# Stage-1 and stage-2 attention on one Trainium2 core: both halves of q and k are copied first, tokens are prepared a unit sooner, their transpose is issued first

## The chip, the cores and the metric

The kernel runs on 1 core of one Trainium2 chip. The metric is the device time of one execution in microseconds (us). A core has TensorE (PE, with its weight loads as PEld), VectorE (DVE), ScalarE (ACT), GpSimd (POOL) and SyncE (SP), which here only issues DMAs. Each engine takes its own instructions strictly in order; engines wait for one another through semaphores.

## The reference

```python
x = x + tanh(g_xattn[0]) * L0_xattn(layernorm(x), ctx)   # 8 heads of 64
x = x + tanh(g_ffn[0])   * L0_ffn(layernorm(x))          # 16 experts, chosen by a Sinkhorn affinity
x = x + tanh(g_xattn[1]) * L1_xattn(layernorm(x), ctx)   # 16 heads of 64
x = x + tanh(g_ffn[1])   * L1_ffn(layernorm(x))          # 2 of 8 experts for each of the 128 samples
# xattn: q = x Wq, k = ctx Wk, v = ctx Wv; softmax(q k^T / 8) v; then Wo and a bias
```

x is 128 samples of 64 tokens of 128 floats, the context 128 x 64 x 96. All is float32.

## The kernel before

A tile is two samples: 128 tokens on the 128 partitions, 64 tiles in all. The program has four parts in a row: the first attention, the expert layer, the second attention and the routed layer. The change lies in the function `attention`, which builds the first and the second attention. In the first (`first` is true) a tile is one unit, 64 units. In the second a tile is two units of eight heads each (G = 2), 128 units; keys come from DRAM, where the expert layer has left them (`keys_ahead`), and the first half of the program has also left the transposed context there (`context_T`).

Each engine runs `body(j)` for j in order. `Unit(j, k)` is the unit j - k, so a positive k is a unit that started k steps ago and a negative k one that is prepared ahead. A unit `opens` if it is the first of its tile: each unit of the first attention, each second one of the second. What the engines do in step j, in their order:

- PE: project q (and in the first attention k) of unit j in two parts (`U0`, `U1`, each in a PSUM bank of its own), V of unit j-2, output product Y of j-5, attention times V (O) of j-4, scores S of unit j. S(j) waits for the copy of q and k (`uc1`, or `uc0` in the second attention) and for `sub` of j-1. For the second attention there is one part.
- ACT: copy of O (j-5); copy of the first part of q and k (j); high half of V (`vh`, j-2); exp (j-1), which waits for `sub`; copy of the second part of q and k (j); high half of the probabilities (`phi`, j-2); then, for the tile of unit j+3, the layer norm (`ln`, into `xn`) and its high half in f16 (`xh`, into `parted[..., 0]`).
- DVE: sum over exp (`den`, j-2) and its reciprocal (`rden`); maximum (`top`) and difference (`sub`) of the scores j-1; low half of V (`vl`, j-2), after `vh`; low half of the normed tokens (`xl`, tile of j+2); in the first attention the high half of the context (`chi`, j+3); the residual (`res`, j-5); norm statistics; in six steps of each of three stretches of the first attention also a part of the arithmetic of the norm (`norm`, stages 0 to 5).
- POOL: probabilities times `rden` (`mul`, j-2); bias added to x; a share of the expert weights' split (first attention); low half of the probabilities (`plo`, j-2), after `phi`; low half of the context (`clo`, tile of j+2).
- SP, in order: weight and input loads of the first attention; store of `context_T`; keys and context of unit j+1 (second attention); transpose of the probabilities `PT` of j-2, which waits for `plo`; transpose of the tokens (`transpose_tokens`, L505 to L512) of j+2, which waits for `xl`, in the first attention also for `clo`.

The values are split into a high and a low f16 half (hi + lo), and products run as three passes. The transposed tokens land in `XT`; PE waits for them (semaphores `xc`) before U of an opening unit. `XT` and `parted` have 4 slots in the first attention and 2 in the second, `xn` has 2. The line of ACT's copies is L640, that of a helper, whatever they copy.

Of the kernel before, what the change touches and what calls it, by code (L numbers as in the profile page):

```python
# [103 lines left out]
def _build(nc, whole, I, out):  # L104
# [190 lines left out]
    def attention(tag, G, Wq, Wk, Wv, Wo, bo, gate, ew=None, rw=None, routing=None):  # L295

        first = ew is not None
        U = NT * G
        INNER = 512 * G
        s = Sems(tag)  # L300
        with ExitStack() as c:
# [148 lines left out]
            with nc.Block() as block:  # L450
                @block.sync
                def _(e):
                    def body(j):
                        a, a2, nx, soon = (Unit(j, k) for k in (0, 2, -1, -2))
                        if first and a.on and a.par == 0:
                            turn = a.j.mod(4)
                            if turn == 0 and a.j.off > 0:
                                n = a.j.div(4)
                                wait(e, s["ew_lo"], n, 2, -2)
                                load_w2(e, n)  # L460
                            elif turn == 2 and (a.j + 2).inside(U):
                                n = (a.j - 2).div(4) + 1
                                wait(e, s["ew_lo"], n, 2, -3)
                                load_w1(e, n)
                        if first and 2 <= j.off < 10:
                            part = 16 * (j.off // 6 + 2)
                            four = slice(4 * j.off + 24, 4 * j.off + 28)
                            e.dma_start(x[:, four, :], xv[:, four, :]).then_inc(s[f"x{part}"], 16)
                            e.dma_start(ctx32[:, four, :], cv[:, four, :]).then_inc(s[f"c{part}"], 16)
                        if first and 24 <= j.off < 24 + NE:  # L470
                            n = j.off - 24
                            with nc.allow_non_contiguous_dma("a small bias, transposed once"):
                                e.dma_start(ew.b1T[:, FT * n:FT * n + FT],
                                            I["L0_ffn_b1"][n].rearrange("(k p) -> p k", p=P)).then_inc(s["b1"], 16)
                        if a.opens and first:
                            on_slot(e, "xc", a)
                            e.dma_start(context_T[bass.ds(a.t.value, 1)].rearrange("o p k -> p (o k)"),
                                        XT[0:DC, a.slot, 2:4].rearrange("p h t -> p (h t)"))\
                             .then_inc(s[f"stored{a.slot}"], 16)
                        if nx.opens and not first and nx.j.off > 0:  # L480
                            load_keys(e, nx)
                            load_context(e, nx)
                        if a2.on:
                            wait(e, s["plo"], a2.j)
                            wait(e, s["O"], a2.j - 2)
                            e.dma_start_transpose(PT[:, a2.par].rearrange("p h k t -> p (h k) t"),
                                                  Ph[:, a2.par].rearrange("p h k t -> p (h k t)"))\
                             .then_inc(s[f"pt{a2.par}"], 16)
                        if soon.opens and (first or soon.j.off > 0):
                            transpose_tokens(e, soon)  # L490
                        if rw is not None:
                            if 8 <= j.off < 18:
                                rw.load_small(e, j.off - 8)
                            if 18 <= j.off < 18 + 2 * NE1:
                                rw.load_expert(e, (j.off - 18) // 2, j.off % 2)
# [18 lines left out]
                    def load_keys(e, a):  # L514
                        wait(e, s["S"], a.j - 3)
                        e.dma_start(KL1[:, a.tp].rearrange("p k l -> p (k l)"),
                                    keys_ahead[bass.ds(a.t.value, 1)].rearrange("o p k -> p (o k)"))\
                         .then_inc(s[f"ul{a.tp}"], 16)
# [115 lines left out]
                @block.scalar  # L634
                def _(e):
                    def body(j):
                        a, a1, a2, a5, later = (Unit(j, k) for k in (0, 1, 2, 5, -3))

                        def copy(to, frm):
                            return e.activation(to, frm, ACT.Copy)  # L640
# [14 lines left out]
                            copy(O32[:, a5.par], psO[:, :, 0:256]).then_inc(s["oc"], 1)  # L655
                        if a.on:
                            projected(0)
                        if a2.on:
                            wait(e, s["V"], a2.j)
                            wait(e, s["O"], a2.j - 4)  # L660
                            copy(vB[:, a2.four, 0].rearrange("p b k -> p (b k)"), psV[:]).then_inc(s["vh"], 1)
                        if a1.on:
                            wait(e, s["sub"], a1.j)
                            e.activation(E[:, a1.four], E[:, a1.four], ACT.Exp, bias=zero_col[:], scale=DH ** -0.5)\  # L664
                             .then_inc(s["exp"], 1)
                        if a.on and first:
                            projected(1)
                        if a2.on:
                            wait(e, s["mul"], a2.j)
                            wait(e, s[f"pt{a2.par}"], turn_of(a2.j, 2, a2.par) - 1, 16)  # L670
# [4 lines left out]
                        if later.opens:  # L675
                            wait(e, s["xl"], later.t - 2)
                            e.activation(xn[:, later.tp, :], tile_of(later.t, x), ACT.Identity, bias=column_of(later.t, nmr),
                                         scale=column_of(later.t, rstd)).then_inc(s["ln"], 1)
                            on_slot(e, "xc", later, -1)
                            wait(e, s["ln"], later.t)  # L680
                            copy(parted[:, later.slot, 0, :], xn[:, later.tp, :]).then_inc(s["xh"], 1)
                    if first:
                        parts = (0, 8, 16, 32, 48, U)
                        for part, (lo, hi) in enumerate(zip(parts, parts[1:])):
                            e.wait_ge(s["nmr"], part + 1)
                            pipeline(e, body, lo - 3, hi - 3, max(lo - 3, 8), hi - 3, 4)
                        for j in range(U - 3, U + 5):
                            body(Step(None, 0, j))
                    else:
                        for name in ("ln", "xh"):  # L690
                            e.sem_inc(s[name], 1)
                        pipeline(e, body, -1, U, 8, U - 3, 4)
                        for j in range(U, U + 5):
                            body(Step(None, 0, j))
                            if j < U + 3:
                                routing["scalar"](e, j - U, psQK[:, 1, :])

                @block.gpsimd
                def _(e):
                    def body(j):  # L700
                        a, a2, soon = (Unit(j, k) for k in (0, 2, -2))
                        if a2.on:
                            wait(e, s["rden"], a2.j)
                            e.tensor_tensor(E[:, a2.four], E[:, a2.four],  # L704
# [28 lines left out]
                    if rw is not None:  # L733
                        rw.clear(e)
                    if first:
                        pipeline(e, body, -2, U + 2, 8, U - 2, 4)
                    else:
                        routing["clear"](e)
                        pipeline(e, body, 0, U + 2, 8, U, 4)
                        routing["gpsimd"](e)  # L740

                @block.vector
                def _(e):
                    def body(j, ahead=()):
                        a, a1, a2, a5, soon, later = (Unit(j, k) for k in (0, 1, 2, 5, -2, -3))
                        by_head = "p (k h) n -> p h k n"

                        if a2.on:
# [19 lines left out]
                        if soon.opens and (first or soon.j.reg is not None or soon.j.off > 0):  # L768
                            wait(e, s["xh"], soon.t)
                            e.tensor_tensor(parted[:, soon.slot, 1, :], xn[:, soon.tp, :], parted[:, soon.slot, 0, :],  # L770
                                            ALU.subtract).then_inc(s["xl"], 1)
                        if first and later.on:
                            on_slot(e, "xc", later, -1)
                            e.tensor_copy(parted[:, later.slot, 2, 0:DC], tile_of(later.t, ctx32)).then_inc(s["chi"], 1)
                        if a5.closes:
                            wait(e, s["Y"], a5.j)
# [16 lines left out]
                    if first:  # L793
# [4 lines left out]
                                    body(Step(i, 4, lo + u), ahead)  # L798

                        e.wait_ge(s["c0"], 16)  # L800
                        for j in range(-3, 0):
                            body(Step(None, 0, j))
                        e.wait_ge(s["x8"], 16)
                        for j in range(4):
# [8 lines left out]
                        for part, lo in ((2, 8), (3, 24), (4, 40)):  # L813
# [4 lines left out]
                                e.wait_ge(s["c48"], 64)  # L818
                            for j in range(lo, lo + NORM_STAGES):
                                body(Step(None, 0, j), (24,) if j < 40 else ())  # L820
                                for stage in ((0, 1), (2,), (3,), (4,), (5,), ())[j - lo]:
                                    norm(part, slice(lo + 8, lo + 24), stage)
                            if lo < 40:
                                for j in range(lo + 6, lo + 8):
# [5 lines left out]
                    else:  # L830
# [3 lines left out]
                        e.wait_ge(s["stats"], 8)  # L834
                        queue_norm(e, s, lnt, 0, late)
                        queue_shift(e, s, 0, late, nmr)
                        e.sem_inc(s["xl"], 1)
                        pipeline(e, body, -1, U, 8, U - 3, 4)
                        pa, pb = psQK[:, 1, :], psS[:, 0, :]
                        routing["vector"](e, -1, pa, pb)  # L840
                        for j in range(U, U + 5):
# [1321 lines left out]
```

## Time and profile before

| | us |
|---|---|
| median of 3 runs | 2038.03 (2034.89 to 2048.37) |
| the profiled execution | 2044.66, its span 2042.9 |
| busy in the span: PE, DVE, ACT, POOL | 1785.4, 1554.4, 1553.0, 671.9 |
| TensorE's granted clock, mean | 0.966 of full speed |

The first attention runs from about 16 to 350 us of the span, the expert layer to about 1370, the second attention to about 1895, the routed layer to the end. Busy shares are means over stages with different limits. "Idle before" an instruction with a releaser says what ended the wait of its engine. Start times and durations of successive instructions on one engine overlap a little, since the next starts while the last drains.

### The profile page before, as it was taken

Reading aid. Unit: us, or ns where it says so; the run is one execution under the profiler, and the core shown is the slowest. Engines: PE = TensorE matmul, PEld = TensorE weight load, DVE = VectorE, ACT = ScalarE, POOL = GpSimd, SP = SyncE. Lnnn points to the kernel's source line nnn. Section 1 sums busy time; section 2 is a strip of 40 time slices with the busy share of each in tenths; the row PEclk is TensorE's granted clock in tenths of the full one; section 3 lists DMA queues with packets and bytes.
Section 4 is the critical chain, followed back from the end, with each engine's and each line's share of the span. In section 5 each row is a group of like instructions: output and inputs, shape, how many; then the busy total and the mean of one; then the engine's idle time right before and its main releaser. Section 6 shows DMA issues by size and latency. Waiting matters only on the chain. (4 is left out here: it accounts for less than half of the span.)

```text
span 2042.9 us, 95028 instructions
## 1 busy us (share of the span) xinstructions
PE 1785.4 (87%) x39513; PEld 1389.3 (68%) x39513; DVE 1554.4 (76%) x3645; ACT 1553.0 (76%) x2637; POOL 671.9 (33%) x921
## 2 busy tenths in 40 slices
PE   3788888788799999999999999967888888888798
PEld 3777777534366666666666666757777777777687
DVE  4788887579688888888888888765777777777654
ACT  3687877466699999999999998856777777777443
POOL 3677777442000000000000000014555555555465
PEclk8899999799799999999999999988999999999799
DMA  6755555379200000000000001005665555555233
GB/s 158 146 114 112 119 113 113 101 270 372 71 13 14 12 14 12 14 12 14 12 14 12 14 12 52 2 24 118 150 156 139 137 141 139 138 146 142 68 114 114
DMA packets 371233, 185.79 MB, mean 91 GB/s; under 512 B 290366, under 2 KB 350822, under 8 KB 371046
## 3 DMA queue, kind: packets, MB, share of 16 engines
q1 hardware_dynamic: 370198, 182.55, 34.4%
q8 instruction: 123, 2.02, 0.4%
q10 hardware_dynamic: 848, 0.71, 0.1%
q14 instruction: 64, 0.52, 0.1%
HBM read 68.95 MB, written 42.86 MB: 55 GB/s over the span
## 5 line engine op out<-in xcount | busy, mean ns | idle before, releaser
L1646 DVE TENSOR_TENSOR h<-g,h 128x1024 f16<-128x1024 f32 x256 | 313.4, 1224 | 137.9 <-ACT h L1571 137.6
L245 PEld LDWEIGHTS psE<-ew,h 128*128 128x128 f16 x6144 | 350.9, 98 | 56.0 <-issue 40.1
L245 PE MATMUL psE<-ew,h 128*128 128x128 f16 x6144 | 365.0, 219 | 12.8 <-DVE eo L1656 6.0
L1566 ACT ACTIVATE g<-psH,eb1T 128x512 f32<-128x512 f32 x512 | 330.3, 680 | 30.5 <-PE psH L245 24.1
L723 POOL TENSOR_TENSOR Ph<-E,Ph 128x512 f16<-128x512 f32 x192 | 222.4, 1159 | 304.1 <-ACT Ph L640 304.1
L1586 POOL TENSOR_TENSOR shared<-shared 128x128 f16<-128x128 f32 x1 | 0.4, 428 | 846.6 <-ACTq L1387 846.6
L1571 ACT ACTIVATE h<-g 128x1024 f16<-128x1024 f32 x256 | 270.6, 1057 | 8.1
L704 POOL TENSOR_TENSOR E<-E,rden 128x512 f32<-128x512 f32 x192 | 200.0, 1042 | 51.2 <-DVE rden L753 50.6
L562 PE MATMUL psQK<-shared 128*64 128x128 f16 x3072 | 114.6, 226 | 76.6 <-DMA shared<-shared 71.6
L245 PE MATMUL psH<-shared,ew 128*128 128x512 f16 x768 | 178.6, 383 | 0.0
L245 PE MATMUL psH<-xg,ew 128*128 128x512 f16 x768 | 176.9, 380 | 0.0
L765 DVE TENSOR_TENSOR vB<-psV,vB 128x512 f16<-128x512 f32 x128 | 88.0, 687 | 107.7 <-ACT vB L640 107.3
L640 ACT ACTIVATE QK<-psQK 128x512 f32<-128x512 f32 x128 | 76.4, 597 | 106.1 <-PE psQK L562 106.0
L664 ACT ACTIVATE E<-E,zero_col 128x512 f32<-128x512 f32 x192 | 137.5, 716 | 22.6 <-DVE E L760 22.1
L562 PEld LDWEIGHTS psQK<-shared 128*64 128x64 f16 x3072 | 93.5, 113 | 89.6 <-DMA shared<-shared 41.1
L590 PE MATMUL psY<-shared 128*64 128x128 f32 x2048 | 137.7, 278 | 5.1 <-ACT shared L640 5.1
L751 DVE TENSOR_REDUCE den<-E 128x8 f32<-128x512 f32 x192 | 129.8, 676 | 13.7 <-ACT E L664 12.1
L760 DVE TENSOR_TENSOR E<-psS,top 128x512 f32<-128x512 f32 x192 | 132.8, 692 | 9.7
L757 DVE TENSOR_REDUCE top<-psS 128x8 f32<-128x512 f32 x192 | 127.2, 663 | 13.6 <-PE psS L622 13.5
L245 PEld LDWEIGHTS psH<-shared,ew 128*128 128x128 f16 x768 | 70.3, 98 | 93.6 <-issue 19.0
L245 PEld LDWEIGHTS psH<-xg,ew 128*128 128x128 f16 x768 | 69.9, 98 | 89.9 <-issue 12.7
L640 ACT ACTIVATE shared<-psO 128x512 f32<-128x512 f32 x192 | 112.4, 586 | 16.1 <-PE psO L607 10.4
(284 smaller groups left out, 3810.9 us busy)
## 6 DMA issues: line engine op xcount, KB each, us to landing
keys_ahead<-shared SPq DMA_DIRECT2D x64, 512.0 KB, 4.9
shared<-keys_ahead SPq DMA_DIRECT2D x64, 512.0 KB, 3.8
rawe<-in_L_ffn_w_dram SPq DMA_DIRECT2D x32, 256.0 KB, 3.1
wb<-rw SPq DMA_DIRECT2D x64, 128.0 KB, 2.0
rows<-places SPq DMA_DIRECT2D x110, 64.0 KB, 2.6
out_dram<-x SPq DMA_DIRECT2D x7, 512.0 KB, 3.2
context_T<-shared SPq DMA_DIRECT2D x64, 48.0 KB, 2.4
PT<-Ph SPq DMA_TRANSPOSE x192, 3.4
```

What stands on the lines that cost most here:

```text
L245: last = e.matmul(to, a, b, start=start and n == 0, stop=stop and n == 2, **flags)
L562: last = e.matmul(psQK[half(m), bank, P * q:P * q + P], w[0:rows, wl, a.g, k, half(m)], moving[:, ml, :], start=n == 0, stop=n == 2)
L590: last = e.matmul(psY[half(b), 0:D], O32[:, a5.par, hp, P * k2 + 64 * b:P * k2 + 64 * b + 64], wo[:, a5.g, k2, hp, :], start=a5.g == hp == ...
L640: return e.activation(to, frm, ACT.Copy)
L664: e.activation(E[:, a1.four], E[:, a1.four], ACT.Exp, bias=zero_col[:], scale=DH ** -0.5)\
L704: e.tensor_tensor(E[:, a2.four], E[:, a2.four], rden[:, a2.par, :].unsqueeze(2).broadcast_to([P, 8, N]), ALU.mult)\
L723: e.tensor_tensor(Ph[:, a2.par, 1].rearrange("p k t -> p (k t)"), E[:, a2.four].rearrange("p h l -> p (h l)"), Ph[:, a2.par, 0].rearrange( ...
L751: e.tensor_reduce(den[:, a2.par, :], E[:, a2.four], AX.X, ALU.add).then_inc(s["den"], 1)
L760: e.tensor_tensor(E[:, a1.four].rearrange(by_head, h=2), scores, top[:].unsqueeze(3).broadcast_to([P, 2, 4, N]), ALU.subtract).then_inc(s[ ...
L1566: e.activation(g32[:, ft, :], psH[:, ft, :], ACT.Gelu_apprx_tanh, bias=b1T[:, a.expert(1) * FT + ft:a.expert(1) * FT + ft + 1]).then_inc(s ...
L1571: e.activation(h[:, 1 - par, 0, ft - 1:ft + 1, :], g32[:, ft - 1:ft + 1, :], ACT.Copy).then_inc(s["h_hi"], 1)
L1646: e.tensor_tensor(h[:, 1 - par, 1, 2 * q:2 * q + 2, :], g32[:, 2 * q:2 * q + 2, :], h[:, 1 - par, 0, 2 * q:2 * q + 2, :], ALU.subtract)\
```

## The change

- ACT copies the second part of q and k right behind the first (first attention), ahead of `vh` and exp.
- Layer norm (`ln`) on ACT is made for the tile of j+4 in place of j+3. Its high half `xh` moves from ACT to DVE: it stands behind `xl` in DVE's step and waits for the `ln` of the same step number. `chi` also goes to j+4, `xl` and `clo` to j+3.
- SP issues the transpose of the tokens of j+2 at the head of its step, ahead of loads, store and `PT`. The keys of the second attention are loaded for j+2 and still ahead of `PT`, the context for j+1 behind it.
- The last two stages of the norm's arithmetic are done in one step. Loops and start counts are shifted to match.

```diff
@@ -451,7 +451,9 @@
                 @block.sync
                 def _(e):
                     def body(j):
-                        a, a2, nx, soon = (Unit(j, k) for k in (0, 2, -1, -2))
+                        a, a2, soon = (Unit(j, k) for k in (0, 2, -2))
+                        if soon.opens and (first or soon.j.off > 0):
+                            transpose_tokens(e, soon)
                         if first and a.on and a.par == 0:
                             turn = a.j.mod(4)
                             if turn == 0 and a.j.off > 0:
@@ -477,17 +479,17 @@
                             e.dma_start(context_T[bass.ds(a.t.value, 1)].rearrange("o p k -> p (o k)"),
                                         XT[0:DC, a.slot, 2:4].rearrange("p h t -> p (h t)"))\
                              .then_inc(s[f"stored{a.slot}"], 16)
-                        if nx.opens and not first and nx.j.off > 0:
-                            load_keys(e, nx)
-                            load_context(e, nx)
+                        if soon.opens and not first:
+                            load_keys(e, soon)
                         if a2.on:
                             wait(e, s["plo"], a2.j)
                             wait(e, s["O"], a2.j - 2)
                             e.dma_start_transpose(PT[:, a2.par].rearrange("p h k t -> p (h k) t"),
                                                   Ph[:, a2.par].rearrange("p h k t -> p (h k t)"))\
                              .then_inc(s[f"pt{a2.par}"], 16)
-                        if soon.opens and (first or soon.j.off > 0):
-                            transpose_tokens(e, soon)
+                        nx = Unit(j, -1)
+                        if nx.opens and not first and nx.j.off > 0:
+                            load_context(e, nx)
                         if rw is not None:
                             if 8 <= j.off < 18:
                                 rw.load_small(e, j.off - 8)
@@ -634,7 +636,7 @@
                 @block.scalar
                 def _(e):
                     def body(j):
-                        a, a1, a2, a5, later = (Unit(j, k) for k in (0, 1, 2, 5, -3))
+                        a, a1, a2, a5, later = (Unit(j, k) for k in (0, 1, 2, 5, -4))
 
                         def copy(to, frm):
                             return e.activation(to, frm, ACT.Copy)
@@ -655,6 +657,8 @@
                             copy(O32[:, a5.par], psO[:, :, 0:256]).then_inc(s["oc"], 1)
                         if a.on:
                             projected(0)
+                            if first:
+                                projected(1)
                         if a2.on:
                             wait(e, s["V"], a2.j)
                             wait(e, s["O"], a2.j - 4)
@@ -663,8 +667,6 @@
                             wait(e, s["sub"], a1.j)
                             e.activation(E[:, a1.four], E[:, a1.four], ACT.Exp, bias=zero_col[:], scale=DH ** -0.5)\
                              .then_inc(s["exp"], 1)
-                        if a.on and first:
-                            projected(1)
                         if a2.on:
                             wait(e, s["mul"], a2.j)
                             wait(e, s[f"pt{a2.par}"], turn_of(a2.j, 2, a2.par) - 1, 16)
@@ -676,20 +678,16 @@
                             wait(e, s["xl"], later.t - 2)
                             e.activation(xn[:, later.tp, :], tile_of(later.t, x), ACT.Identity, bias=column_of(later.t, nmr),
                                          scale=column_of(later.t, rstd)).then_inc(s["ln"], 1)
-                            on_slot(e, "xc", later, -1)
-                            wait(e, s["ln"], later.t)
-                            copy(parted[:, later.slot, 0, :], xn[:, later.tp, :]).then_inc(s["xh"], 1)
                     if first:
                         parts = (0, 8, 16, 32, 48, U)
                         for part, (lo, hi) in enumerate(zip(parts, parts[1:])):
                             e.wait_ge(s["nmr"], part + 1)
-                            pipeline(e, body, lo - 3, hi - 3, max(lo - 3, 8), hi - 3, 4)
-                        for j in range(U - 3, U + 5):
+                            pipeline(e, body, lo - 4, hi - 4, max(lo - 4, 8), hi - 4, 4)
+                        for j in range(U - 4, U + 5):
                             body(Step(None, 0, j))
                     else:
-                        for name in ("ln", "xh"):
-                            e.sem_inc(s[name], 1)
-                        pipeline(e, body, -1, U, 8, U - 3, 4)
+                        e.sem_inc(s["ln"], 1)
+                        pipeline(e, body, -2, U, 8, U - 4, 4)
                         for j in range(U, U + 5):
                             body(Step(None, 0, j))
                             if j < U + 3:
@@ -698,7 +696,7 @@
                 @block.gpsimd
                 def _(e):
                     def body(j):
-                        a, a2, soon = (Unit(j, k) for k in (0, 2, -2))
+                        a, a2, soon = (Unit(j, k) for k in (0, 2, -3))
                         if a2.on:
                             wait(e, s["rden"], a2.j)
                             e.tensor_tensor(E[:, a2.four], E[:, a2.four],
@@ -733,7 +731,7 @@
                     if rw is not None:
                         rw.clear(e)
                     if first:
-                        pipeline(e, body, -2, U + 2, 8, U - 2, 4)
+                        pipeline(e, body, -3, U + 2, 8, U - 3, 4)
                     else:
                         routing["clear"](e)
                         pipeline(e, body, 0, U + 2, 8, U, 4)
@@ -742,7 +740,7 @@
                 @block.vector
                 def _(e):
                     def body(j, ahead=()):
-                        a, a1, a2, a5, soon, later = (Unit(j, k) for k in (0, 1, 2, 5, -2, -3))
+                        a, a1, a2, a5, soon, later = (Unit(j, k) for k in (0, 1, 2, 5, -3, -4))
                         by_head = "p (k h) n -> p h k n"
 
                         if a2.on:
@@ -769,8 +767,11 @@
                             wait(e, s["xh"], soon.t)
                             e.tensor_tensor(parted[:, soon.slot, 1, :], xn[:, soon.tp, :], parted[:, soon.slot, 0, :],
                                             ALU.subtract).then_inc(s["xl"], 1)
+                        if later.opens and (first or later.j.reg is not None or later.j.off > 0):
+                            wait(e, s["ln"], later.t)
+                            on_slot(e, "xc", later, -1)
+                            e.tensor_copy(parted[:, later.slot, 0, :], xn[:, later.tp, :]).then_inc(s["xh"], 1)
                         if first and later.on:
-                            on_slot(e, "xc", later, -1)
                             e.tensor_copy(parted[:, later.slot, 2, 0:DC], tile_of(later.t, ctx32)).then_inc(s["chi"], 1)
                         if a5.closes:
                             wait(e, s["Y"], a5.j)
@@ -798,7 +799,7 @@
                                     body(Step(i, 4, lo + u), ahead)
 
                         e.wait_ge(s["c0"], 16)
-                        for j in range(-3, 0):
+                        for j in range(-4, 0):
                             body(Step(None, 0, j))
                         e.wait_ge(s["x8"], 16)
                         for j in range(4):
@@ -818,7 +819,7 @@
                                 e.wait_ge(s["c48"], 64)
                             for j in range(lo, lo + NORM_STAGES):
                                 body(Step(None, 0, j), (24,) if j < 40 else ())
-                                for stage in ((0, 1), (2,), (3,), (4,), (5,), ())[j - lo]:
+                                for stage in ((0, 1), (2,), (3,), (4, 5), (), ())[j - lo]:
                                     norm(part, slice(lo + 8, lo + 24), stage)
                             if lo < 40:
                                 for j in range(lo + 6, lo + 8):
@@ -834,8 +835,9 @@
                         e.wait_ge(s["stats"], 8)
                         queue_norm(e, s, lnt, 0, late)
                         queue_shift(e, s, 0, late, nmr)
-                        e.sem_inc(s["xl"], 1)
-                        pipeline(e, body, -1, U, 8, U - 3, 4)
+                        for name in ("xh", "xl"):
+                            e.sem_inc(s[name], 1)
+                        pipeline(e, body, -2, U, 8, U - 4, 4)
                         pa, pb = psQK[:, 1, :], psS[:, 0, :]
                         routing["vector"](e, -1, pa, pb)
                         for j in range(U, U + 5):
```

## Rows read from the trace of the kernel before

**Rows 1.** Query by line L765 (`vl`, once a unit): first and last start, three stretches
```profile
L765 DVE TENSOR_TENSOR shared<-psV,shared x16: 680/691/693, 112.0 to 187.7; 128x512 f16<-128x512 f32 x16
...
L765 DVE TENSOR_TENSOR shared<-psV,shared x12: 691/691/693, 292.9 to 346.0; 128x512 f16<-128x512 f32 x12
...
1420.00:1820.00 400.00, 66.05 (x96) 0.99 0.57 142
```
**Rows 2.** Waits by total (us, times, longest), first attention, 110 to 270 us
```profile
PE psS L622 <- ACT shared L640: 24.0, 32, 1.6
```
**Rows 3.** Waits, second attention, 1450 to 1800 us
```profile
PE psQK L562 <- DMA shared<-shared: 43.0, 40, 1.2
```
**Rows 4.** Timeline (start us, duration us, engine) of the first attention, one step
```profile
205.64 0.69 DVE L760 TENSOR_TENSOR E<-psS,top 128x512 f32<-128x512 f32 x1
...
207.09 0.71 ACT L664 ACTIVATE E<-E,zero_col 128x512 f32<-128x512 f32 x1
...
207.70 0.59 ACT L640 ACTIVATE shared<-psQK 128x512 f32<-128x512 f32 x1
...
208.18 0.63 ACT L640 ACTIVATE Ph<-E 128x512 f16<-128x512 f32 x1
...
208.23 0.20 DVE L774 CAST shared<-ctx 128x96 f16 x1
208.35 0.34 DVE L778 SCALAR_TENSOR_TENSOR x<-psY,tanh_g,x 128x128 f32 x1
...
208.70 0.49 ACT L677 ACTIVATE xna<-x,nmr,rstd 128x128 f32 x1
...
209.04 0.67 DVE L751 TENSOR_REDUCE den<-E 128x8 f32<-128x512 f32 x1
```
**Rows 5.** Timeline of the second attention, from one pair of units
```profile
1706.77 0.35 DVE L778 SCALAR_TENSOR_TENSOR x<-psY,tanh_g,x 128x128 f32 x1
...
1707.47 0.67 DVE L751 TENSOR_REDUCE den<-E 128x8 f32<-128x512 f32 x1
...
1709.00 0.69 DVE L760 TENSOR_TENSOR E<-psS,top 128x512 f32<-128x512 f32 x1
...
1709.72 0.72 ACT L664 ACTIVATE E<-E,zero_col 128x512 f32<-128x512 f32 x1 [0.23 <-DVE E L760]
...
1710.35 0.61 ACT L640 ACTIVATE Ph<-E 128x512 f16<-128x512 f32 x1
...
1710.87 0.48 ACT L677 ACTIVATE shared<-x,nmr,rstd 128x128 f32 x1
...
1711.04 1.15 POOL L723 TENSOR_TENSOR Ph<-E,Ph 128x512 f16<-128x512 f32 x1 [1.55 <-ACT Ph L640]
```
**Rows 6.** Timelines of POOL and DVE, 17 to 19 us and at 83 us
```profile
17.46 0.51 POOL L709 TENSOR_TENSOR x<-x,bo_rep 128x128 f32<-128x128 f32 x1
...
17.59 0.46 DVE L774 CAST shared<-ctx 128x96 f16<-128x96 f32 x1
...
18.50 0.40 POOL L729 TENSOR_TENSOR shared<-ctx,shared 128x96 f16<-128x96 f32 x1
...
18.60 0.37 DVE L774 CAST shared<-ctx 128x96 f16<-128x96 f32 x1
...
82.62 1.15 POOL L723 TENSOR_TENSOR Ph<-E,Ph 128x512 f16<-128x512 f32 x1 [0.47 <-ACT Ph L640]
...
83.00 0.81 DVE L267 TENSOR_SCALAR lnt<-lnt 128x16 f32<-128x16 f32 x1
```
**Rows 7.** Query by line L774 (`chi`, the nearest row to the moved `xh`): min/median/max ns
```profile
L774 DVE CAST shared<-ctx x64: 196/202/461, 15.8 to 342.1; 128x96 f16<-128x96 f32 x36, 128x96 f16 x28
```
**Rows 8.** DVE's timeline, the `den` of an early unit and the 14th after it
```profile
33.40 0.69 DVE L751 TENSOR_REDUCE den<-E 128x8 f32<-128x512 f32 x1 [0.51 <-ACT E L664]
...
113.56 0.67 DVE L751 TENSOR_REDUCE den<-E 128x8 f32<-128x512 f32 x1
```
**Rows 9.** Busy times by stretch (PE, PEld, DVE, ACT, POOL), PEclk, DMA, GB/s
```profile
80.00:90.00 10.00, 6.34 (x158) 5.67 (x156) 6.20 (x14) 4.10 (x9) 5.64 (x8) 0.71 0.87 166
```

## The prediction

> **What bounds the kernel now.** I read the slices of the page first. Only the two attentions run the changed code, so I left the expert and the routed layer alone and asked each attention for its period. The line that runs once a unit gives it: in the first attention 11 intervals in 53.1 us, 4.83 us a unit, and 15 in 75.7 us, 5.05 a unit, where part of the norm's arithmetic falls in [rows 1]. In the second attention 96 units in 400 us are 4.17 a unit, 8.33 a pair, that is a tile [rows 1].
>
> Then the waits. In the first attention PE stands before the scores in each of 32 units for ACT's copy of q and k, 24.0 us or 0.75 a unit [rows 2]. The timeline shows why: that copy stands behind exp on ACT (exp 207.09, copy 207.70) [rows 4]. In the second attention PE stands 40 times, about once a pair, for the transposed tokens, 43.0 us, 1.07 each [rows 3]: their transpose stands behind that of the probabilities on SP. So each attention has one wait that the change goes at, and the page of itself would promise 0.75 x 64 + 1.07 x 64, some 116 us. The question is what is late next.
>
> **The change part by part.** The earlier copy of q and k removes the wait before the scores, and it costs exp nothing: exp started 0.76 us after the difference had ended (205.64 + 0.69 = 206.33, exp 207.09) [rows 4], and with the copy out of its way it can start at once. The earlier transpose no longer stands behind the wait for `plo` and its transpose; its own inputs are ready a step ahead, some 4 us, against a lateness of 1.07 [rows 1, 3]; that wait goes too. Keys and context keep waits that are long satisfied and are issued, as before, about a unit or more before use; I put them, the shifted slots, and the shifted starts and ends at nothing. PE's work covers them; uncovered, they would give back at most the 1.07 a pair.
>
> The part that I cost as a loss is the high half `xh`. It used to run on ACT, a step ahead of the DVE instruction that needed it. Now DVE itself waits, in step j, for the `ln` that is the LAST instruction of ACT's step j. Behind the waiting DVE instruction stand the residual, the statistics and then `den`, `rden`, `top`, `sub` of the next step; for that `sub` wait exp on ACT and the scores on PE. This closes a ring: sub -> exp -> phi -> ln (ACT) -> xh -> (chi) -> res -> stats -> den -> top -> sub. Its length is a lower bound for the period, and I add it up from start to start, with den at 0:
>
> - den to sub 1.53 (1707.47 to 1709.00), sub ends at 2.22, exp starts 0.03 later at 2.25, phi 0.63 later at 2.88, ln 0.52 later at 3.40 and ends at 3.88 [rows 5]. DVE can start xh at 3.91.
> - `plo` on POOL starts 0.69 after phi (1710.35 to 1711.04), at 3.57, and lasts 1.15, to 4.72 [rows 5]. I take the same for the first attention, where phi and ln keep the same distance, 0.52 [rows 4].
> - res to the next den, with the statistics between, takes 0.69 (208.35 to 209.04) and 0.70 (1706.77 to 1707.47) [rows 4, 5].
>
> How long does xh take? The nearest row is the cast of the context: 0.20 us in the median, up to 0.46 [rows 7]; with a third more columns about 0.22. The cast's successor starts 0.12 after it (208.23 to 208.35) [rows 4], so that of xh about 0.14 after it. But xh always starts while plo runs, 0.34 after it began. The trace shows what becomes of such a DVE instruction: a cast that starts at 17.59 ends at 18.05, where POOL's addition ends at 17.97; one from 18.60 ends at 18.97, POOL's at 18.90; a TENSOR_SCALAR on 16 columns takes 0.81, from 83.00 to 83.81, where plo ends at 83.77 [rows 6]. All end 0.04 to 0.08 after POOL's. So xh should take until about 4.79 and release its successor at about 4.72, not 4.05.
>
> The Trainium skill says why, in "SBUF — State Buffer", section "SBUF: two separate sides": DVE and GpSimd share one pair of ports as an exclusive lock, held for the whole instruction, and a DVE operation in a 2-port mode waits for it. By that rule, which rows 6 bear out, xh is held; without it the free reckoning below would stand. The rule speaks against moving a copy onto DVE at just this place.
>
> In the first attention chi follows, another cast. POOL's own next instruction is `clo`, 0.37 to 0.40, which queues right behind plo; the case at 18.50 shows that POOL gets its turn between two held DVE instructions [rows 6]. Then clo ends at about 5.09, chi's successor res starts there, and den at 5.09 + 0.69 = 5.78. If chi slips in first, res starts at 4.84 and den at 5.53. If neither cast is held, xh and chi take 0.14 + 0.12: 3.91 + 0.26 + 0.70 = 4.87. I take 5.78, since both casts have a row that shows it.
>
> In the second attention only the even step has ln and xh, and no chi: 4.72 + 0.70 = 5.42; not held 3.91 + 0.14 + 0.70 = 4.75. The odd step goes on once exp has ended: 2.25 + 0.72 + 0.03 = 3.00. A pair takes 8.42, or not held 7.75.
>
> **The sum.**
> - First attention, the last 48 units: (5.78 - 4.83) x 48 = +45. The norm's arithmetic shows in the period as about 15 x 0.22 = 3 us for each part; in the ring it is exposed entirely, but no longer held up by plo (83.00 [rows 6]), and should cost about the same, 0.
> - First attention, 14 units before: they took 80.2 us, 5.73 each, since inputs were late and the norm came in full [rows 8]. 14 x 5.78 = 81 plus two parts of the norm at 3 to 4 us is 88: +8. Transposes issued sooner may give up to all of it back, so its bounds are 0 and +10.
> - Second attention: (8.42 - 8.33) x 62 pairs = +6, bounds -5 and +12.
>
> Together +59 on the profiled execution of 2044.7, so 2104. That one lies 6.6 above the median of the runs; against the median I predict 2097. With chi not held the sum is (5.53 - 4.83) x 48 = 34 in place of 45: 2086. PE, which needs 8.33 - 1.07 = 7.26 a pair and 4.83 - 0.75 = 4.08 a unit, then has 1.1 to 1.7 us idle in every turn of the ring.
>
> **Rivals.**
> - xh is not held (faster). The ring is still there: 4.87 in the first attention, +2 in all; early units -5 for the transposes; (7.75 - 8.33) x 62 = -36. Sum -39: 2038 - 39 = 1999. For it: the median of 64 casts is 0.20. Against it: those stand where POOL is idle or just behind an instruction that waited in their place, and those that did meet POOL were held [rows 6, 7]. It decides by x, the time at which xh's successor starts: the change is 48 (x + 0.12 + 0.69 - 4.83) + 62 (x + 3.70 - 8.33) = 110 x - 480, which is zero at x = 4.36, about half way between not held (4.05) and held (4.72).
> - The ring does not close, and PE's own work bounds both attentions: 4.08 and 7.26 a pair, -116 with all units, about 1925. This needs DVE to find ln done ahead. ACT's order forbids it: exp of the same step waits for DVE's sub. Very small.
> - Gains and losses cancel (the same): xh is held in every second unit only, mean x 4.39, which gives +2, and with the early units at -5 to +8 a time of 2035 to 2048.
> - Slower yet: PE idles over 1 us in each unit of the first attention, and its granted clock falls from 2.4 to 1.2 GHz at times, as in a stretch of this trace where PE was busy 6.34 of 10 us and the mean was 0.71 of full speed [rows 9]. A unit wholly at half speed would take PE up to 8.2 in place of 4.08, 2.4 above the ring: 12 such units, +29, 2126.
>
> **How the numbers follow.** The ring with held casts has a chance of 0.71, with clock losses on top 0.06, cancelling 0.07, not held 0.12, the ring open 0.04. The likeliest gives 2097; its own range is 2075 to 2115 (chi held or not, the early units 0 to +10, the second attention -5 to +12). The 8-in-10 range leaves out the two fast cases and the end of the clock's: 2040 to 2125. A measurement of this kernel can tell about 1% from no change. From the same cases: faster 0.16, same 0.08, slower 0.76.
>
> **What would show it.** In the profile after: PE waits no more for ACT's copy before the scores, but for the `sub` of DVE; DVE's xh is a CAST 128x128 whose mean is near 0.9 us, not 0.2, and its idle before is released by ACT's ln; the waits of PE for the transposed tokens are gone; L765 has a period of about 5.7 in the first attention and about 8.4 a pair in the second. I am wrong if xh's mean is near 0.2 us (then the first rival), if DVE shows no wait on ln (the second), or if the first attention is not longer.

## The result and the profile after

| | before | after |
|---|---|---|
| median | 2042.15 us (4 runs) | 2090.07 us (4 runs, 2085.56 to 2092.29) |
| ratio to before | | 1.0233, 95% interval 1.019 to 1.0277 |
| span of the profiled execution | 2042.9 | 2083.8 |

The change made the kernel 2.3% slower, 48 us by the medians; 2097 was forecast.

Where did it go? The line of `vl` runs once a unit, so its first and last start measure each attention. It is L763 after and L765 before; the answers to the query by line, after first, then before:

```profile
L763 DVE TENSOR_TENSOR vB<-psV,vB x128: 640/681/693, 1410.7 to 1952.2; 128x512 f16<-128x512 f32 x128
L763 DVE TENSOR_TENSOR shared<-psV,shared x64: 678/680/692, 36.8 to 402.0; 128x512 f16<-128x512 f32 x64
```
```profile
L765 DVE TENSOR_TENSOR vB<-psV,vB x128: 639/691/693, 1372.2 to 1911.4; 128x512 f16<-128x512 f32 x128
L765 DVE TENSOR_TENSOR shared<-psV,shared x64: 680/691/693, 37.6 to 361.5; 128x512 f16<-128x512 f32 x64
```

The first attention takes 365.2 us from its first to its last `vl` in place of 323.9, +41.3; the second 541.5 in place of 539.2, +2.3. That is more than the 40.9 between the two spans; what lies between the attentions gave a little back. The two spans differ by less than the medians, since the profiled execution of before (2044.66) lies above its median and that of after (2085.56) is the fastest of the four.

The waits that the change went at are gone, and others stand there. Waits after, first attention, 110 to 270 us (engine, line, released by; us, times, longest):

```profile
ACT E L668 <- DVE E L758: 57.2, 26, 2.9
POOL E L702 <- DVE rden L751: 49.5, 27, 3.0
...
PE psS L624 <- DVE E L758: 27.0, 25, 1.7
...
DVE shared L773 <- ACT xna L679: 13.8, 27, 1.0
```

and second attention, 1450 to 1800 us:

```profile
ACT E L668 <- DVE E L758: 90.2, 77, 2.1
...
DVE shared L773 <- ACT shared L679: 48.1, 41, 2.3
...
PE psS L624 <- DVE E L758: 40.4, 40, 1.0
```

PE waited for ACT's copy before the scores [rows 2]; now it waits for DVE's `sub`, 1.08 us each time, in 25 of the 28 units. The wait for the transposed tokens [rows 3] is not in the list at all. DVE waits in nearly every unit for ACT's `ln` (L679 feeding L773), and ACT and POOL wait for DVE: three engines that wait for one another in a circle.

One turn of the circle, timeline after, 206 to 212 us. The stretch answers to [rows 4]:

```profile
206.18 0.66 DVE L749 TENSOR_REDUCE den<-E 128x8 f32<-128x512 f32 x1
...
207.66 0.69 DVE L758 TENSOR_TENSOR E<-psS,top 128x512 f32<-128x512 f32 x1
...
208.39 0.72 ACT L668 ACTIVATE E<-E,zero_col 128x512 f32<-128x512 f32 x1 [2.02 <-DVE E L758]
208.45 0.69 PE L624 MATMUL psS<-shared 64*64 64x64 f32 x32 [0.85 <-DVE E L758]
...
209.02 0.61 ACT L642 ACTIVATE Ph<-E 128x512 f16<-128x512 f32 x1
209.54 0.48 ACT L679 ACTIVATE xna<-x,nmr,rstd 128x128 f32 x1
209.71 1.16 POOL L721 TENSOR_TENSOR Ph<-E,Ph 128x512 f16<-128x512 f32 x1 [0.55 <-ACT Ph L642]
...
210.05 0.90 DVE L773 CAST shared<-xna 128x128 f16<-128x128 f32 x1 [0.74 <-ACT xna L679]
...
210.83 0.36 POOL L727 TENSOR_TENSOR shared<-ctx,shared 128x96 f16<-128x96 f16 x1
210.87 0.39 DVE L775 CAST shared<-ctx 128x96 f16<-128x96 f32 x1
...
211.18 0.34 DVE L779 SCALAR_TENSOR_TENSOR x<-psY,tanh_g,x 128x128 f32<-128x128 f32 x1
...
211.84 0.66 DVE L749 TENSOR_REDUCE den<-E 128x8 f32<-128x512 f32 x1
```

Follow it from den to den: 5.66 us. xh (L773) starts when ln has ended, 3.87 after den, while plo (POOL L721) has run for 0.34; it is held (it has started and does not end) until 210.95, 0.08 after plo's end. Then clo takes its turn at 210.83, and chi, issued at 210.87, is held to 211.26, 0.07 after clo's end. xh's duration in the whole kernel:

```profile
L773 DVE CAST shared<-xna x64: 227/903/936, 16.0 to 380.5; 128x128 f16<-128x128 f32 x64
L773 DVE CAST shared<-shared x63: 227/897/911, 1404.1 to 1926.6; 128x128 f16<-128x128 f32 x63
```

The minimum, 0.23, is what it takes when it is alone.

### The profile page after: what moved, and what is told of

Its sections match the earlier page's. It is cut to its first block and busy times, and to the rows that moved or that the text cites. A ratio compares the mean times of both kernels' runs of the same rounds, so it can differ in the third digit from the quotient of the medians.

```text
span 2083.8 us, 95099 instructions
## 1 busy us (share of the span) xinstructions
PE 1800.2 (86%) x39513; PEld 1379.7 (66%) x39513; DVE 1658.0 (80%) x3772; ACT 1510.6 (72%) x2510; POOL 674.0 (32%) x921
## 5 line engine op out<-in xcount | busy, mean ns | idle before, releaser
L721 POOL TENSOR_TENSOR Ph<-E,Ph 128x512 f16<-128x512 f32 x192 | 222.7, 1160 | 160.4 <-ACT Ph L642 160.3
L624 PE MATMUL psS<-shared,QK 64*64 64x64 f32 x4096 | 90.7, 226 | 65.8 <-DVE E L758 62.5
L592 PEld LDWEIGHTS psY<-shared 128*64 128x64 f32 x2048 | 115.4, 138 | 31.9 <-DVE x L779 24.4
L624 PEld LDWEIGHTS psS<-shared,QK 64*64 64x64 f32 x4096 | 76.6, 137 | 76.1 <-issue 70.6
L642 ACT ACTIVATE Ph<-E 128x512 f16<-128x512 f32 x192 | 118.0, 615 | 5.0 <-POOL E L702 2.9
```

The lines of the kernel that those rows point to most:

```text
L592: last = e.matmul(psY[half(b), 0:D], O32[:, a5.par, hp, P * k2 + 64 * b:P * k2 + 64 * b + 64], wo[:, a5.g, k2, hp, :], start=a5.g == hp == ...
L624: last = e.matmul(psS[half(b), hp, N * k:N * k + N], QK[half(hp), a.par, 0, k, half(b)], keys[half(hp), half(b)], start=True, stop=True)
L721: e.tensor_tensor(Ph[:, a2.par, 1].rearrange("p k t -> p (k t)"), E[:, a2.four].rearrange("p h l -> p (h l)"), Ph[:, a2.par, 0].rearrange( ...
```

## The experiments

For each kernel I read two numbers besides the time: the mean distance of successive `den` in the first attention (its last 50 of 63), and that of a pair in the middle of the second. The ratio is to the kernel before on the same chip. The median of e7 is of two executions, the others are of four to seven.

| kernel | median us | ratio, 95% interval | unit, first | pair, second |
|---|---|---|---|---|
| before | 2042 | 1 | 4.94 | 8.32 |
| after | 2090.07 | 1.0233 (1.019 to 1.0277) | 5.69 | 8.54 |
| b1_copy_only | 2033.88 | 0.9959 (0.994 to 0.9978) | 4.84 | 8.31 |
| b2_transpose_only | 1973.46 | 0.9661 (0.9639 to 0.9684) | 4.86 | 7.32 |
| e1_xh_on_act | 1966.25 | 0.9619 (0.9597 to 0.964) | 4.81 | 7.26 |
| e2_ln_before_phi | 1974.7 | 0.966 (0.9639 to 0.968) | 4.74 | 7.50 |
| e3_plo_waits | 2021.95 | 0.9904 (0.9874 to 0.9934) | 5.08 | 8.01 |
| e4_ln_before_exp | 1976.83 | 0.9674 (0.9655 to 0.9694) | 5.02 | 7.28 |
| e5_chi_first | 2078.67 | 1.0184 (1.0157 to 1.021) | 5.56 | 8.54 |
| e6_chi_on_act | 1940.52 | 0.9506 (0.9483 to 0.9529) | 4.42 | 7.23 |
| e7_short_split | 1940.11 | 0.9496 (0.947 to 0.9521) | 4.39 | 7.22 |

### One part undone: xh back on ACT

```diff
# e1_xh_on_act, against after (ACT, behind ln; DVE's copy removed)
+                            on_slot(e, "xc", later, -1)
+                            wait(e, s["ln"], later.t)
+                            copy(parted[:, later.slot, 0, :], xn[:, later.tp, :]).then_inc(s["xh"], 1)
...
-                            e.tensor_copy(parted[:, later.slot, 0, :], xn[:, later.tp, :]).then_inc(s["xh"], 1)
```

> The changed kernel with xh back on ACT, behind ln; DVE's xl of the next step waits for it, a step later. Theory (ring over DVE's wait for ln, plus xh held by POOL): the ring is open, PE's own work bounds, about 4.1 to 4.4 us a unit in the first attention and 7.3 to 7.5 a pair in the second, so about 1950 to 1965 us. Rival (the loss comes from the sooner preparation, the slots or the order on SP, not from where xh runs): stays near 2090.

1966.25 us, 124 less than after. The rival falls: everything else of the change is still in this kernel, and it is 3.8% faster than before. The pair is 7.26, just under what was expected, and it is PE's own work: PE is busy for 341.7 of the 350 us from 1450 to 1800. The unit of the first attention is not: 4.81 in place of 4.1 to 4.4. That is taken up below.

### Two parts alone: the copy, the transpose

```diff
# b1_copy_only, against before (ACT)
                             projected(0)
+                            if first:
+                                projected(1)
...
-                        if a.on and first:
-                            projected(1)
# b2_transpose_only, against before (SP: from the step's end to its head)
+                        if soon.opens and (first or soon.j.off > 0):
+                            transpose_tokens(e, soon)
```

> The kernel before with only the second copy of q and k moved up on ACT. Theory: PE's wait of 0.75 a unit goes and nothing takes its place: 4.1 to 4.4 a unit in the first attention, the second unchanged, about 2010 us. Rival (the transposed tokens or DVE are late next): 4.7 to 4.8 a unit, 2035 or more.

> The kernel before with only the tokens' transpose moved to the head of SP's step, everything prepared as before. Theory: PE's wait of 1.07 a pair goes: 7.3 to 7.5 a pair, the first attention nearly unchanged, about 1985 us. Rival (the transpose then waits for xl of its own step, or other work is late next): 8.0 or more a pair, 2025 or more.

The transpose alone gives 69 us, where 57 were expected, nearly all of it in the second attention (474.9 us from its first `den` to its last in place of 542.0; 323.8 in place of 327.0 in the first): 7.32 a pair with nothing prepared sooner. The preparation a unit ahead was not needed for it. The copy alone gives 9 us, where 32 were expected; something else is late at 4.8, the time that its rival gave. Two things stand in its trace: from 110 to 270 us PE waits 18 times, 14.1 us in all, for the transposed tokens, as the rival said, and units of 3.83 and 5.56 follow each other as they do in e1, which is taken up below. In e1 that wait of PE is gone and the unit is still 4.81. The two gains add up to 78, and e1, with both of them, gives 76: so the whole loss of the change is where xh runs, 124 us between e1 and after, and it hid a gain of 76.

### The hold and the ring, apart

```diff
# e3_plo_waits, against after (POOL, ahead of plo)
+                        after_xh = Unit(j, -4)
+                        if after_xh.opens:
+                            wait(e, s["xh"], after_xh.t)
# e4_ln_before_exp, against after: the block of ln on ACT moved from behind phi to ahead of exp
# e2_ln_before_phi, against after: the same block moved to ahead of phi
```

In e3 POOL's loop of the second attention also ends four steps sooner and the rest is written out, since the last four units have no tile to wait for.

> The changed kernel in which POOL's plo waits for xh of the same step, so that no POOL instruction runs while xh does; the order of ACT and DVE, and so the ring, is left. Theory (ring and hold are two terms): xh drops from 0.90 to about 0.23 us, the ring is 4.87 a unit and 7.75 a pair, about 2000 us. If the ring alone made the loss: near 2090. If the hold alone did: as fast as without the ring, about 1955.

> The changed kernel with ln ahead of exp on ACT, where ACT stands idle for DVE's sub: DVE no longer waits for anything that hangs on its own sub. Theory: the ring is gone with xh still on DVE, DVE shows no wait for ln, 4.1 to 4.4 a unit and 7.3 to 7.5 a pair, about 1950 to 1965 us. Rival (DVE is full with xh, its own work bounds): 4.6 or more a unit in the first attention, about 1975.

> The changed kernel with ln ahead of phi on ACT. Theory: the ring loses phi (0.52) and xh, then at about 3.4 after den, runs before plo has begun, so it is not held and takes about 0.23: 4.3 to 4.4 a unit in the first attention, 7.3 to 7.5 a pair in the second, about 1955 to 1970 us. Rival (xh is slow by itself, 0.9 us, whatever POOL does): it stays at 0.9 and the time is some 40 us above that.

e3 keeps POOL off while xh runs and leaves the order of ACT and DVE. The time falls by 68 us. xh in e3, query by line:

```profile
L776 DVE CAST shared<-xna x64: 219/227/391, 15.8 to 345.6; 128x128 f16<-128x128 f32 x64
L776 DVE CAST shared<-shared x63: 226/227/229, 1371.1 to 1864.4; 128x128 f16<-128x128 f32 x63
```

0.23 in the median in both attentions: xh is not slow by itself, it was held. The ring is still there, and DVE still waits for ln, timeline of e3:

```profile
1608.05 0.23 DVE L776 CAST shared<-shared 128x128 f16<-128x128 f32 x1 [1.10 <-ACT shared L679]
1608.26 0.35 DVE L782 SCALAR_TENSOR_TENSOR x<-psY,tanh_g,x 128x128 f32 x1
...
1608.36 1.16 POOL L724 TENSOR_TENSOR Ph<-E,Ph 128x512 f16<-128x512 f32 x1 [1.10 <-DVE shared L776]
```

Its pair is 8.01 where 7.75 was expected; its even steps take 4.84 and 5.08 by turns, not 4.75. In both, res follows xh by 0.21 or more and not by 0.14. In the longer one `sub` also follows `top` by 0.79 in place of 0.70, and xh starts 0.13 after ln's end in place of 0.03. I did not find why, and both are in the pair of after as well. The odd steps take 3.01 and 3.09 by turns, not 3.00.

e4 leaves xh on DVE and cuts the ring: ln runs where ACT stands idle for `sub`. In the second attention DVE shows no wait for ln any more, the pair is 7.28, and the time falls by another 45. So of the 113 us between after and e4, 68 go with the hold and 45 with the ring that is left without it. From first `den` to last the two attentions take 366.1 and 544.5 us in after, 330.6 and 514.7 in e3, 326.8 and 474.1 in e4: the hold cost about as much in the one as in the other, and nearly all of the 45 is in the second.

The first attention of e4 missed its forecast. DVE waits for ln only three times there, but the unit is 5.02, above the 4.81 of e1, and the numbers that came, 5.02 and 1976.83, are those of the rival. DVE is busy for 152.0 of the 160 us from 110 to 270, in part because it is held: xh, 0.22 in the median, takes 0.54 in the mean. Units of 4.02 and 5.84 follow each other; a long one, timeline of e4:

```profile
207.43 1.17 POOL L718 TENSOR_TENSOR ew<-rawe,ew 128x512 f32 x1
207.76 0.98 DVE L768 TENSOR_TENSOR shared<-xna,shared 128x128 f16<-128x128 f32 x1
208.60 1.16 POOL L721 TENSOR_TENSOR Ph<-E,Ph 128x512 f16<-128x512 f32 x1
208.67 1.18 DVE L773 CAST shared<-xna 128x128 f16<-128x128 f32 x1
```

Here xl is held by POOL's subtraction for the expert weights and xh by plo. So e4 cuts the ring in both attentions, and takes the hold away only in the second.

In e2, ln ahead of phi shortens the ring by 0.52, and xh, now earlier than plo, is 0.23 long: the hold is gone and a shorter ring is left, in which DVE still waits for ln 61 times in the second attention. The pair is 7.50, at the upper end of the forecast; the unit of the first attention is 4.74 in place of 4.3 to 4.4, and the time 1974.7 lies above the 1955 to 1970 expected. The rival, xh slow by itself, falls here too.

### chi behind xh

```diff
# e5_chi_first, against after: DVE's cast of the context stands ahead of xh
```

> The changed kernel with the cast of the context (chi) ahead of xh on DVE. Theory: chi is done while DVE would wait for ln, 0.20 us, and is not held by POOL's clo any more; the first attention's unit falls by 0.3 us, about 15 us in all, 2075; the second is unchanged. Rival (chi's 0.39 lay beside other work): no change, 2090.

2078.67: 11 us less, where 15 were expected; from first `den` to last the first attention is 8.7 shorter. The unit is 5.43 and 5.76 by turns; only in every second one did it fall by 0.3. In the other POOL subtracts the expert weights: xl is held for 0.97, chi through plo for 1.17 (222.05 to 223.22), and xh by clo for 0.42. The second attention, which has no chi, did not move. That chi's hold by clo is a term of its own is shown; that it is worth 0.3 in each unit is not.

### What bounds the first attention once PE's wait is gone

Distances of successive `den` in e1 and e6, units 12 to 23, read from DVE's timeline:

```
e1_xh_on_act    4.02 5.42 3.83 5.57 3.91 5.64 3.87 6.02 3.90 5.65 3.88 5.71
e6_chi_on_act   4.24 4.62 3.71 4.60 3.78 4.68 3.76 5.04 3.78 4.68 3.75 4.75
```

A mean near 4.8 is in fact 3.9 and 5.65 by turns. The long one, timeline of e1, DVE and POOL:

```profile
217.51 1.16 POOL L722 TENSOR_TENSOR ew<-rawe,ew 128x512 f32 x1
217.88 0.94 DVE L772 TENSOR_TENSOR shared<-xna,shared 128x128 f16<-128x128 f32 x1
218.63 1.21 POOL L725 TENSOR_TENSOR Ph<-E,Ph 128x512 f16<-128x512 f32 x1
218.74 1.16 DVE L776 CAST shared<-ctx 128x96 f16 x1
219.80 0.36 POOL L731 TENSOR_TENSOR shared<-ctx,shared 128x96 f16<-128x96 f16 x1
219.82 0.34 DVE L780 SCALAR_TENSOR_TENSOR x<-psY,tanh_g,x 128x128 f32 x1
```

In every second step POOL subtracts the expert weights (1.16). xl is held to its end, 0.94 in place of 0.28, and comes out just late enough that plo has begun, and chi is held through all of plo: 1.16 in place of 0.20. Two kernels test that:

```diff
# e6_chi_on_act, against e1: chi leaves DVE; on ACT, ahead of exp
+                        if first and later.on:
+                            on_slot(e, "xc", later, -1)
+                            copy(parted[:, later.slot, 2, 0:DC], tile_of(later.t, ctx32)).then_inc(s["chi"], 1)
# e7_short_split, against e1 (POOL)
-                                e.tensor_tensor(lo, rawe[:, turn // 2], hi, ALU.subtract).then_inc(s["ew_lo"], 1)
+                                e.tensor_copy(lo, rawe[:, turn // 2]).then_inc(s["ew_lo"], 1)
```

> e1_xh_on_act with the cast of the context (chi) on ACT, where ACT waits for DVE's sub. In e1 the first attention's units alternate between 3.9 and 5.65 us: where POOL subtracts the expert weights (1.16), xl is held to its end and chi is then held through plo, 1.16. Theory (the shared port is what bounds the first attention once PE's wait is gone): chi's hold goes, xl's stays, the long unit falls from 5.65 to about 4.4 to 4.6, the mean from 4.77 to about 4.2, and the time from 1966 to about 1935 to 1945. Rival (PE or ACT is late at 4.7 anyway): 1960 or more.

> e1_xh_on_act with POOL's subtraction in the expert weights' split replaced by a plain copy (0.61 in place of 1.16 us; the low halves of the weights are then wrong). Theory: xl is no longer held, chi comes before plo, the alternation of 3.9 and 5.65 goes and all units take about 3.9 to 4.1 in the first attention, about 35 to 40 us less than e1, near 1930. Rival (the alternation has another cause): as e1, 1966.

Both land at 1940, 26 us under e1. In e6 POOL's work is what it was and the long unit falls by 1.0, from 5.65 to 4.68: chi's hold, and the little that chi takes by itself. What is left of the alternation is put down to xl, still held for 0.94 in the long unit (208.21). The mean is 4.42, where about 4.2 was expected. In e7 POOL's instruction is shorter and the units are 3.9 to 4.6 with no alternation, though chi is still on DVE; chi takes 0.20 again, and xl 0.32 in the mean in place of e1's 0.58. So it was POOL's subtraction, through the port, that stood at 4.8. In b1 the same rows stand (chi 0.40 to 0.51 in the mean in place of 0.20), and it is the likeliest reason that b1 gained 9 us and not 32; PE's wait for the transposed tokens is another, and no run has parted them there. e7's time was expected ten lower; its stretches with the norm's arithmetic still take 5 to 6 a unit.

e6 computes the same as the kernel before and beats both: 4.9% under before, 7% under after.

## Why the prediction was right

The forecast was slower, 2097, and the time was 2090.07, by the mechanism named. The 7 us between them understate the miss: the forecast was +59 on a median of 2038.03, and the median of before, with a fourth run, is 2042.15, so the change is +48. Several terms were also off and cancelled in part, which is luck. Point by point:

- **The ring.** Predicted from rows of before: xh can start 3.91 after den. Measured 3.87. exp, phi and ln follow each other as in [rows 5], and the distance of plo from phi is 0.69 again.
- **The hold.** xh was put at about 0.88 (3.91 to 4.79); it is 0.90. [rows 6] carried this: three instructions that met POOL, against a median of 0.20 over 64 casts, nearly all of which did not. The Trainium skill's rule of an exclusive lock ("SBUF — State Buffer", section "SBUF: two separate sides") holds here, and e3 shows it from the other side: with POOL kept off, 0.23.
- **chi held again by clo.** Predicted for all units, 5.78 a unit; measured 5.66 to 5.75 in about half of them, 5.8 to 7.0 in the others; the 45 between the first 13 and the last five take 5.91 in the mean, with the norm's arithmetic in it. e5 bears out the cause. The prediction read POOL's turn between two held DVE instructions off the case at 18.50; the first of the two is not in [rows 6], but it stands in the timeline of before, held by POOL's cast:

```profile
17.93 0.60 POOL L717 CAST ew<-rawe 128x512 f16<-128x512 f32 x1
18.18 0.50 DVE L770 TENSOR_TENSOR shared<-xna,shared 128x128 f16<-128x128 f32 x1
```

- **The first attention's sum, 45 + 8.** It was 41.3 in place of 53. The step "14 units before: they took 80.2 us" miscounted: [rows 8] are 13 distances apart, not 14. With 13 the ring gives 75, with the norm 82, and +2 in place of +8; measured 81.5 to 80.2, +1.3. The other 50 distances are 284.6 to 246.8, +37.8 in place of 45, since the last five units prepare no tile and run at 3.3 to 4.2, below before's: I had charged them the ring.
- **The second attention, +6.** The pair is 8.54, not 8.42, against 8.32: 62 such pairs alone would make +14. The total is +2.3. By the `den`s, 51 pairs in the middle are 12.0 us longer, the last five steps 5.1 shorter, for the same reason as in the first attention, and the first 20 steps 4.4 shorter, for which no run shows the cause. Errors that cancel: here it was luck that +6 came near.
- **The waits of [rows 2] and [rows 3] go, and their gain is swallowed by the ring.** Right, and the size of what was swallowed is now known: 76 us.
- **The rival in which PE's own work bounds**, "about 1925": with the ring cut the kernels come to 1966 and 1977. Its step "4.08 a unit" was wrong: before PE, the holds at the port that DVE and POOL share bound the first attention (e6, e7). The 4.08 was the period less PE's wait, 4.83 - 0.75, as if nothing else were late next, and xl's holds, visible in the trace of before, were left out. The expectations of e1, e2, e4 and b1 carried the same error. xl before (min/median/max ns), query by line:

```profile
L770 DVE TENSOR_TENSOR shared<-xna,shared x64: 281/286/1000, 16.7 to 346.6; 128x128 f16<-128x128 f32 x64
```

- **The clock rival** did not come: PE stands idle for about 1.3 us of each 5.7 in the first attention (223.14 busy in 290), and the granted clock holds at 0.98. Stretches after (PE, PEld, DVE, ACT, POOL, PEclk, DMA, GB/s):

```profile
100.00:390.00 290.00, 223.14 (x7764) 195.12 (x7766) 256.65 (x560) 180.21 (x349) 187.53 (x249) 0.98 0.47 98
```

## What to carry to other kernels

Before an instruction moves to another engine, write down what it waits for in the same step, what stands behind it, and whether what it waits for itself hangs on this engine; if so, the moved instruction closes a ring, and the ring's length bounds the new period from below even where no engine is full. Here it was 5.66 us with DVE busy for 256.65 of 290, holds included. A small instruction's price is its duration only if nothing else holds its port at that moment: look for rows where the two engines did meet, since a median hides them. And a change of several parts that loses as a whole is worth taking apart: here one copy, moved to this place, cost 124 us and covered a gain of 76.

## What was not expected of the hardware

- A DVE instruction of 0.20 us was held for 1.16 by one POOL instruction that began 0.11 before it, and here POOL and DVE took strict turns: xl, plo, chi, clo (e1, from 217.88). Two short DVE instructions in a row can so be held by two POOL instructions in a row, 2.10 us (0.94 + 1.16) for what takes 0.48 (0.28 + 0.20) when POOL is idle.
- Such a hold depends on tenths of a microsecond: with POOL's instruction at 0.61 in place of 1.16 (e7) nearly all of it was gone, 26 us.
- `sub` follows `top` on DVE by 0.70 or 0.79 by turns with no releaser shown. It stays open.
